# Where the last five chunks of context values are projected: inside the long attention's loop, or before it

## What is computed

```python
    ...
    x = x + _L0_ffn_ref(_layernorm(x, axis=-1), L0_ffn_gate_w1, ...)
    x = x + _L1_xattn_ref(_layernorm(x, axis=-1), ctx_768, L1_xattn_Wq, ...)
    ...

def _L1_xattn_ref(query, key_value, Wq, bq, Wk, bk, Wv, bv, Wo, bo):
    ...
    q = (query @ Wq + bq).reshape(B, Nq, H, D).transpose(0, 2, 1, 3)
    k = (key_value @ Wk + bk).reshape(B, Nkv, H, D).transpose(0, 2, 1, 3)
    v = (key_value @ Wv + bv).reshape(B, Nkv, H, D).transpose(0, 2, 1, 3)
    attn = jnp.einsum('bhqd,bhkd->bhqk', q, k) * scale
    attn = jnp.clip(attn, -CLAMP, CLAMP)
    attn = jax.nn.softmax(attn, axis=-1)
    ...
    x = jnp.einsum('bhqk,bhkd->bqhd', attn, v).reshape(B, Nq, Cq)
    return x @ Wo + bo
```

## Time and profile before

| | us |
|---|---|
| median of 3 runs | 349.13 |
| lowest, highest run | 346.26, 349.15 |
| the profiled execution | 348.56 |
| its span, first to last instruction | 346.7 |

### The profile page before, as it was taken

How to read it: one execution, slowest core, us unless ns; L and a number is a source line. 1 busy time by engine, 2 the same in 40 slices (tenths; PEclk the granted TensorE clock), 3 DMA queues, 4 the chain that set the end, 5 groups by cost and what they waited for, 6 DMA issues and landing times.

```text
span 346.7 us, 7813 instructions
## 1 busy us (share of the span) xinstructions
PE 271.3 (78%) x3060; PEld 164.9 (48%) x3061; DVE 233.9 (67%) x585; ACT 174.1 (50%) x316; POOL 50.7 (15%) x175
## 2 busy tenths in 40 slices
PE   0009595878786997799999996787999999849854
PEld 0003323335343876744445553274666666535742
DVE  4888999968789957559534445675667677165734
ACT  3749896765637655130002000566777878702530
POOL 3213030800000200200002002012222222110002
PEclk9999878999999999899999999887899999965975
DMA  6990000000006998770000000000000000000001
GB/s 173 265 368 14 1 2 0 1 3 2 2 2 136 219 223 212 218 309 16 0 0 0 2 0 0 1 0 2 5 5 4 5 5 6 6 1 0 4 2 30
DMA packets 6320, 19.41 MB, mean 56 GB/s; under 512 B 1156, under 2 KB 2692, under 8 KB 5252
## 3 DMA queue, kind: packets, MB, share of 16 engines
q1 hardware_dynamic: 6277, 18.82, 19.8%
HBM read 12.07 MB, written 0.26 MB: 36 GB/s over the span
## 4 chain that ended last, share of the span: by engine, by line
PE 57%; DVE 28%; ACT 7%; issue 3%; POOL 3%; DMA 1%; DVEq 0%; ACTq 0%; POOLq 0%
PE PS L1121 53%; DVE sm L763 5%; DVE sm L700 3%; DVE yq L772 2%; DVE big L821 2%; DVE w L923 2%; POOL rstd L325 2%; ACT sa L418 1%; DVE sm L922 1%; POOL yq L349 1%; DVE yq L830 1%; PE PS L1315 1%; PE PS L1236 1%; ACT yq L418 1%; DVE tern L712 1%
## 5 line engine op out<-in xcount | busy, mean ns | idle before, releaser
L1075 DVE TENSOR_REDUCE sm<-PS 128x1 f32<-128x512 f32 x64 | 43.1, 688 | 21.4 <-PE PS L1121 20.6
L600 ACT ACTIVATE yq<-PS,sm 128x512 f32<-128x512 f32 x44 | 29.8, 687 | 10.6 <-PE PS L1121 9.9
L325 POOL TENSOR_TENSOR rstd<-veps,mhalf 128x1 f32<-128x1 f32 x24 | 12.6, 549 | 142.7 <-DVE veps L635 142.7
L1121 PE MATMUL PS<-sa,w 128*32 128x36 f32 (+1 forms) x320 | 30.8, 280 | 2.4 <-ACT w L553 2.4
L1121 PE MATMUL PS<-yq 128*128 128x384 f32 x96 | 31.1, 486 | 0.0
L1121 PE MATMUL PS<-yq,big 99*128 99x128 f16 x256 | 26.1, 226 | 4.7 <-issue 2.0
L418 ACT ACTIVATE big<-PS,cols,sm 128x512 f32<-128x512 f32 (+1 forms) x32 | 27.1, 887 | 2.2 <-PE PS L1121 2.1
L530 ACT COPY xT<-PS 128x512 f32<-128x512 f32 x5 | 2.9, 588 | 49.9 <-PE PS L1315 49.9
L1121 PE MATMUL PS<-big,yq 96*128 96x512 f16 x64 | 25.6, 405 | 2.6 <-ACT yq L418 2.6
L1121 PE MATMUL PS<-diag,ones 128*128 128x128 f32 x14 | 4.1, 379 | 29.9 <-DVE diag L680 20.8
L1121 PEld LDWEIGHTS PS<-yq,big 99*128 99x128 f16 x256 | 17.3, 100 | 17.4 <-issue 14.8
(11 more groups left out here) (251 smaller groups left out, 558.2 us busy)
## 6 DMA issues: line engine op xcount, KB each, us to landing
big<-yq SPq DMA_DIRECT2D x24, 256.0 KB, 5.2
cx<-ctx_in SPq DMA_DIRECT2D x8, 384.0 KB, 10.2
w<-w_in SPq DMA_DIRECT2D x9, 256.0 KB, 5.1
yq<-w_in SPq DMA_DIRECT2D x1, 2304.0 KB, 10.7
wa<-wa_in SPq DMA_DIRECT2D x1, 1156.0 KB, 17.9
sa<-wx_in SPq DMA_DIRECT2D x1, 768.0 KB, 13.8
rows<-rows_in SPq DMA_DIRECT2D x1, 580.0 KB, 15.6
tern<-rows_in SPq DMA_DIRECT2D x1, 512.0 KB, 8.9
```

Of the source, the lines that this page charges most:

```text
L325: pool.tensor_tensor(rstd[:, t:t + 1], veps[:, t:t + 1], mhalf[:, t:t + 1], ALU.pow)\
L600: nc.scalar.activation(pt(i), PS[:, ST_BANK[i % 2], :], ACT.Exp, scale=s1(M_ES))\
L1075: V.tensor_reduce(s1(M_MX + i % 8), PS[:, S_BANK[i % 3], :], AX, ALU.max, negate=True)\
L1121: return nc.tensor.matmul(o, lhsT, rhs, start=start, stop=stop, **kw)
```

## The change

The third part of the values leaves the loop. Chunks 11, 12 and 13 stand behind the register load and ahead of the transposes; chunks 14 and 15 behind the query products and ahead of the loop. On ScalarE the copies stand ahead of the copy to `xT`, and behind the last head queries. Their banks are 5 and 4 in place of 6 and 5, since bank 6 takes feed-forward sums. No instruction is added or taken away.

```diff
@@ -179,13 +179,13 @@
-                  tuple((c, 5 + c % 2) for c in range(11, NCH)))
+                  tuple((c, 4 + c % 2) for c in range(11, NCH)))
...
-        VALUE_STEPS = [(b, r) for b in range(3) for r in range(1, R)][:len(VALUES[2])]
+        VALUES_AHEAD = 3
...
@@ -567,6 +567,8 @@
             nc.scalar.activation(s1(M_EXP0), s1(M_Z4), ACT.Exp)
+            for step in range(VALUES_AHEAD):
+                context_values(2, step)
             rows_to_features(3)
...
@@ -586,12 +588,11 @@
             last_heads(2)
             last_heads(3)
-
+            for step in range(VALUES_AHEAD, len(VALUES[2])):
+                context_values(2, step)
 
             for n in range(R * B + LAG_T):
                 b, r = n // R, n % R
-                if (b, r) in VALUE_STEPS:
-                    context_values(2, VALUE_STEPS.index((b, r)))
...
```

## The result

| | before | after |
|---|---|---|
| median us (20 runs each) | 349.73 | 347.53 |
| lowest, highest | 346.26, 351.58 | 343.81, 349.28 |
| profiled execution, its span | 348.56, 346.7 | 345.71, 343.9 |

The ratio after to before is 0.9934, with a 95% interval of 0.9908 to 0.996: 0.4 to 0.9% faster, some 1.4 to 3.2 us. The single runs of either kernel are spread over some 5.4 us, more than the effect, so the stage itself tells more than the totals.

A forecast was written before the change was run, and what follows sets the result against it. TensorE was taken to bound most of the program, its order holding the chain at the loop's entry. 2.1 us won less 0.4 left 1.7, giving 346.9 or 347.4 and, halfway, 347.2 us; range 344.8 to 350.3.

The forecast's parts named there:

- Chunks 11 to 13 at no cost: In TensorE's idle time between feed-forward products and last transpose: three chunks take 3.15 us, cost 0, about a microsecond of cover.
- Chunks 14 and 15 at no cost: Behind the query products: first scores move to 225.55, but VectorE takes no maxima before 228.07, so cost 0.
- The first maxima: At the long attention's entry: with no chunks in front on TensorE, the transposed maxima start 2.01 us earlier.
- The first cast and the first transposed scores: Behind the transposed maxima: ScalarE's cast starts 2.10 us earlier, at the low clock; first transposed scores at 233.75.
- Up to step 13: From first transposed scores to step 13's scores: low clock costs 0.4 us, leaving 1.7 us of gain.
- What is won at the entry is kept: A loop that TensorE fills does not catch up, so the entry's gain lasts to the end.
- The dense part: Loop from step 13: 5.1 us of low clock, as before, losing 2.1 us at 0.40 per us.
- Rival A: Clock stays up under the query products, saving 1.06 us at the first; gain 2.8 us, time 346.1; chance 0.24.
- Rival B: Clock stays low in the loop, 13.0 us from step 13: 1.4 us slower, 350.3; chance 0.17.
- Rival C: Something else holds the transposed maxima and only GpSimd's start counts: gain 0.4 us, time 348.5; chance 0.09.

The follow-up runs named there:

- five ahead: Changed kernel with all five chunks ahead of the transposes, none behind the query products; ratio to the kernel before 0.9945 (0.9901 to 0.9988).
- filled kernel after: Changed kernel plus extra matmuls, results unread, in TensorE's idle time at the loop's entry: 17 behind scores 1 to 6, 9 behind 8, 10, 12; ratio 0.9909.
- four and five ahead: Two kernels: the changed kernel with four or all five chunks, instead of three, ahead of the transposes; ratios 0.9944 and 0.9945.
- four ahead with fillers: Changed kernel with four chunks ahead of the transposes plus extra unread matmuls at the loop's entry (22 and nine); ratio 0.9831, median 344.25 us.
- the other kernel that was profiled twice: Kernel before with only chunk 15 moved one step later, behind the first transposed maxima; ratios 0.9938 and 0.9897.

## Why the prediction was right

The forecast was 1.7 us of gain in the profiled execution's own terms, 347.2 us and no measurable change at 1%. Measured were 347.53 us, and 2.0 us in the stage itself. That the times agree to 0.3 us is in part luck: the forecast was counted from a median before of 349.13 us in 3 runs, which was 349.73 in 20, so the gain by medians was 2.2 us and not the 1.9 that 347.2 stands for. The mechanism was forecast, and came, step by step, with one stretch that was guessed. Point by point:

- **Chunks 11 to 13 at no cost**: right, last transpose at the same 4.57 us. They took 2.89 us and not 3.15, so not even the first transpose was late (3.04 us behind the feed-forward's end, 3.03 before). They started 0.16 us ahead of the last product's end in the profile, so the register load held up nothing. The cover was larger than the microsecond that the prediction gave it, as five ahead showed.
- **Chunks 14 and 15 at no cost**: right. VectorE's first maxima started at 228.08 against 228.07 before.
- **The first maxima**: 2.01 us were predicted and 21.48 - 19.52 = 1.96 measured. The reading on which it rests, that TensorE's order and not the data held the chain, is shown by the wait for GpSimd that stands there now, and by the kernel in which chunk 15 alone moved behind the maxima. One row was misread on the way, without weight in the sum: the 6.47 us of TensorE from 227.70 are 37 records, five scores and four chunks of 8, not five; chunk 11 had run ahead of them, at 226.02.
- **The first cast and the first transposed scores**: 2.10 predicted, at the low clock, 23.25 - 21.20 = 2.05 measured, at the low clock.
- **Up to step 13**: 1.7 predicted, 27.47 - 25.84 = 1.63 measured.
- **What is won at the entry is kept**: right. 2.00 us are left at step 19 (35.37 - 33.37) and 2.01 at the loop's end.
- **The dense part**: mis-sized twice. It was taken at 5.1 us of low clock, as before, which was a guess; in both profiles of the change it was low from step 13 for about 3.6 us, up to the scores of step 15. And its price was taken at 0.40 us per us, by setting steps 13 to 15 at the low clock (3.49 us) beside steps 17 to 19 at the full one (2.08). The same steps 13 to 15 take 2.37 us at the full clock in the filled kernel after (241.75 - 239.38), so the two pairs were not alike, and the price is (3.49 - 2.37) / 3.49 = 0.32. The low clock in the kernel before cost 1.4 us and not 2.1. The price stood on both sides of the forecast and cancelled out; the length did not. From step 13 to step 19 the kernel after takes 7.53 us in place of 7.90, and these 0.37 us, less the 0.07 that were missing at step 13, are the 0.3 us by which the stage gained more than the forecast. The rows of the filled kernel:

```profile
239.38 0.38 PE L1122 MATMUL PS<-big,yq 96*128 96x512 f16 x1
239.98 0.39 PE L1122 MATMUL PS<-yq,big 99*128 99x128 f16 x4 [0.21 <-issue]
240.30 0.65 PE L1122 MATMUL PS<-yq,cst 128*32 128x64 f32 x32
...
241.75 0.39 PE L1122 MATMUL PS<-big,yq 96*128 96x512 f16 x1
```

- **Rival A**, the full clock under the query products, did not come: 0.50 there in both profiles of the change. One chunk more ahead brings it (four and five ahead, and four ahead with fillers). What the rival gives was well sized: 1.06 us at the first query copy against 0.96 measured.
- **Rival B**, slower, did not come in the change. Its mechanism is real: with two chunks left in the loop the low clock lasted 15.8 us, and took 1.0 of 1.7 us.
- **Rival C**, hidden anyway, is out by the timeline: the transposed maxima wait for GpSimd now.

The Trainium skill's rule in the prediction, that activity releases the throttle ("TensorE: Matmul & The Clock Gate", Part 1, What's actually happening), has the direction right where a fourth chunk or fillers were added: the clock was 1.00 under the query products with the one and at the loop's entry with the other, where the change had 0.50. Behind the change's own three chunks it was 0.50 all the same, so the rule alone would have given the wrong rival.

What stays open: why the clock is low for longer behind the loop with four and five chunks ahead, where 0.8 of their 0.9 us are lost again in the profiles, and whether they lose it in every execution; the intervals of their totals are too wide to say. The kernel before was profiled once, so how its low stretches vary is known only by the mean clock of its runs.

## What to carry to other kernels

Where a chain waits for one engine and the data had been ready for a while, look for what stands in front of the waiting instruction in that engine's own order: moving one item behind it was worth as much here as moving all of them away, though only part of that was the place and the rest went with the clock. Before work is taken out of a stretch, read the granted clock of the stretch behind it, since work that looks like a burden may be what keeps TensorE at 2.4 GHz; idle places then are worth filling even with matmuls whose results nobody reads. Where runs scatter by more than the effect, count times from a common event inside the profile: the columns here repeat to 0.03 us in the change and to 0.1 us in the other kernel that was profiled twice. And follow the gain to the end of the program: what four and five chunks ahead won in the loop was lost behind it in their profiles.

## What the runs showed of the hardware

- In the kernel before the clock fell to 0.50 at 228.3 behind query products that had ended 4.9 us earlier, though TensorE had run a chunk and three scores in between; in the change at the same place, with 1.22 of 3.20 us busy (225 to 228.2). With fillers in that place it stayed at 1.00 (224 to 256). In neither of the two had TensorE stood idle throughout.
- Two steps of the loop's dense part, 13 to 15, took 3.49 us in the kernel before and 3.62 in the change at the low clock, and 2.37 with the fillers at the full one: the low clock cost a third of the time there, not half. The rows show two reasons: the 32 records of the outputs take 1.08 us at the low clock and 0.65 at the full one, less than twice, and at the full clock TensorE waits 0.21 us ahead of a group for which it does not wait at the low one.
- Matmuls at a low price: 31 extra ones of 128x512 cost nothing measurable where TensorE was idle (with 22 of them ahead of the transposed maxima these come at 18.33 us, without them at 18.32), and the kernel that has them is the fastest of the study.
- TensorE's load of the flags into its sequencer ran at 206.7 us, 5.9 us ahead of the end of the last product in front of it, and in the change the chunks behind the load did not wait for it.
- The scatter of one kernel's times goes with its clock: runs of the kernel before with a mean granted clock of 0.926 to 0.932 took 346.2 to 347.4 us, those with 0.908 to 0.918 took 348.3 us and more.
